# Multi-head projections between the first two latent groups, with the work of maxima, low parts and normalisation spread anew

## The chip, the core and the metric

The kernel runs on one core of one Trainium2 chip. Its time is the device time of one execution in microseconds (us), and the figure compared is the median of several runs. The profile is of one further execution.

## The reference

The input `x` has 8 batches of 256 rows of 256 features, in float32. It is normalised by row (a layernorm without weights) to `xn`, and two branches start from there:

- a latent attention with 16 heads, each with 16 content and 64 rotary features: `c_q = xn @ w_dq.T`, `c_kv = xn @ w_dkv.T`; queries and keys from these (rotary keys from `xn` directly), scores scaled by `1/sqrt(80)`, causal softmax, values, and the output weights: `s`;
- an ordinary attention with 16 heads of 16 features on `rmsnorm(xn)`, added to `xn` as a residual, and behind it a mixture of 8 experts of which each row takes two: `g = silu(...)`.

The result is `x + s * g`. Everything is float32; where the kernel splits a number into a high part that TensorE reads in one pass and a low remainder, the two add up to it.

## The kernel before

A program of one core, with an order written out by hand for each of the five engines; all waits are semaphores. First come the weights (they are multiplied out and split into high and low parts, to about 28 us), then the eight batches of both attentions and the routing (to about 600 us), then the experts. The change touches the first two parts.

A batch `b` passes three stages on TensorE. They overlap the engines' other work, and the stages of neighbouring batches are interleaved:

- **P1(b), the projections** (`stage_p1`, line 764, with `p1_with_m1`, line 957): thirteen units, in the order of `UNITS` (line 51): content queries and keys `nq`, `nk`, the rotary ones in four groups of four heads `q0` to `k3`, the multi-head ones `mq`, `mk`, and the latent values `v`. Each is twelve matmuls into one PSUM bank (`BANK`); a unit waits until its bank's last content was taken. After `nq` come the last values of the batch before and small transposes, after `k0` `to_tokens`, after `k1` `back`, after `k2` `project` (lines 714 to 741: the heads' way into tokens and through the output weights). After `k3` the first two heads of the maxima's scores.
- **T2(b-1), the multi-head attention** of the batch before (`stage_t2`, line 919, through `heads`, line 839), and in it the latent scores of batch `b` from which only row maxima are taken (`max1`, line 814): head `h + 2` behind the scores of head `h`. At its end the sixteen maxima are transposed (`max_t1`).
- **T1(b), the latent attention** (`stage_t1`, line 882), and in it in the same way the multi-head scores for their maxima (`max2`, line 830), in steps of heads, two of them ahead.

VectorE makes the rope products (`products`, line 1532: two instructions a unit, times cosine and times sine), POOL adds them (`rope_sums`, line 593), SyncE sends the sums into `qt` and `kt` by DMA (`place_rope`, line 440), and ScalarE rounds them there for the maxima's scores (`rounded`, line 1186). ScalarE also keeps `nq` and `nk`, takes all exponentials (`exps`, line 1251), and works strictly in the order of its program: P1's roundings stand ahead of T2's exponentials. For the multi-head queries and keys VectorE scales a unit (`mha_scale`, line 1545), ScalarE takes the high part (`mha_high`), VectorE the low part (`mha_low`, line 1554); SyncE stores the parts in HBM (`store_mha`, twelve DMAs: each high part goes to two places) and loads them back in the layout of the scores (`load_mha`, four DMAs for each half of the heads), once the scores of the batch before have let the half go.

All these pieces pass through one staging ring `stg` of five slots. `place` (line 98) gives each piece the next slot, in the order of `STAGED` (line 53), and the count at which its last user's DMAs have landed; who writes into a slot waits for that count.

The row of latent maxima goes from PSUM through `mt` (ScalarE, `max_t1`, line 1166) into the row `MROW` of `qt` by a DMA that SyncE issues (`row1`, line 410) between the two halves of `load_mha`. VectorE takes the maxima with two reducing instructions a head (`maxima`, line 1590). Between its products stand the normalisation of the heads behind the attention (`normalise` in `close_heads`) and routing steps (`position_steps`, `gate_steps`), put there by number: `after = {1: ..., 6: ...}` in `batch`, line 1601. The layernorm of `x` is applied for batch 0 ahead of its P1, and for the other seven behind the first seven product pairs of P1(0) (line 1761).

Of the kernel before, what the change touches and what calls it, by code (L numbers as in the profile page):

```python
# [23 lines left out]
F32 = mybir.dt.float32  # L24
# [19 lines left out]
G = 4  # L44
# [67 lines left out]
def build(nc, x, w_cols, w_dq, w_uqr, w_dkv, w_ukv, w_out, w_o, w_ln1, w_ln2, w_r, w_experts,  # L112
          cosines, sines, ident, mask, upper, route_c, slots, ones, out):
    ctx = ExitStack()
    with ctx:
# [276 lines left out]
        def _(sp):  # L392
# [17 lines left out]
            def row1(b):  # L410
                sp.wait_ge(mte1, b + 1)
                sp.dma_start(qt[MROW:MROW + 1, :, :], mt[:, :]).then_inc(md1, 16)

# [33 lines left out]
            def zero_rows():  # L447
                sp.wait_ge(clear, 2)
                for e in range(2):
                    sp.dma_start(mha_d[0, e, MROW2:ST, :, :], qt2[MROW2:ST, e, :, :].bitcast(F32)).then_inc(mzd, 16)  # L450

            def store_mha(b, a):
                for name, parts, ready in (((("mqh", (0, 1), hi2), ("mql", (2,), s2d)),
                                            (("mkh", (0, 2), hi2), ("mkl", (1,), s2d)))[a]):
                    s, _, _ = place(b, name)
                    sp.wait_ge(ready, 2 * b + a + 1)
                    for k in parts:
                        for e in range(2):
                            sp.dma_start(mha_d[a, e, D * k:D * (k + 1), :, :].rearrange("d (j t) s -> (d j) t s", t=2),  # L459
                                         stg[e * ST:(e + 1) * ST, s, :, :]).then_inc(sl[s], 16)  # L460

            def load_mha(b, t):
# [9 lines left out]
            def stage_p1(b, between):  # L472
# [11 lines left out]
                between()  # L484
                for t in range(2):
                    wait(sp, mrd[t], 64 * b)
                store_mha(b, 0)
                store_mha(b, 1)

            stage_p1(0, zero_rows)  # L490
# [3 lines left out]
            row1(0)  # L494
            for b in range(last):
# [4 lines left out]
                stage_p1(b + 1, lambda: store_s(b))  # L500
                load_mha(b + 1, 0)
                row1(b + 1)
# [64 lines left out]
        def _(pool):  # L567
# [116 lines left out]
        def _(pe):  # L684
# [79 lines left out]
            def stage_p1(b, after):  # L764

                free = dict(q0=(ex1, 16 * b), k0=(ex1, 16 * b), q1=(nkd, 2 * b + 1), k1=(nkd, 2 * b + 2),
                            q2=(roped, 8 * b + 1), k2=(roped, 8 * b + 2), q3=(roped, 8 * b + 3),
                            k3=(roped, 8 * b + 4), mq=(roped, 8 * b + 5), mk=(roped, 8 * b + 6), v=(roped, 8 * b + 7))
                for name in UNITS:
# [5 lines left out]
                    else:  # L775
                        wait(pe, *free[name])
                    if name == "mq" and b == 0:
                        pe.wait_ge(wdone, N_DIRECT)
# [25 lines left out]
            def max_t1(b):  # L804

                wait(pe, roped, 8 * b + 8)
# [1134 lines left out]
```

## Time and profile before

| what | us |
|---|---|
| median of 3 runs (lowest, highest) | 864.14 (859.2, 868.65) |
| profiled execution | 858.59 |
| its span, first to last instruction | 856.9 |
| busy in it: TensorE matmuls | 756.2 (88%) |
| TensorE weight loads (beside the matmuls) | 677.5 (79%) |
| VectorE | 556.7 (65%) |
| ScalarE | 437.9 (51%) |
| POOL | 378.7 (44%) |
| mean granted clock of TensorE, as a share of 2.4 GHz | 0.914 |

All engines run beside each other, so busy times do not add up to the span. Matmuls are pipelined and the ends that the profile gives them are modelled: a TensorE that is busy throughout need not be at its peak. The granted clock is either 1.00 or 0.50, and a value between is a mean over a stretch. Other names: PEld is the weight load, DVE VectorE, ACT ScalarE, SPq the instruction by which SyncE issues a DMA.

### The profile page before, as it was taken

The numbers are of one execution on the slowest core, as the hardware profiler recorded it, in microseconds if no ns is written. First come the engines' busy times: TensorE is split into PE (matmuls) and PEld (weight loads), VectorE is DVE, ScalarE is ACT, GpSimd is POOL, SyncE is SP. The second block draws the span as 40 slices with busy tenths as digits, with TensorE's granted clock in tenths as the row PEclk, the third lists the DMA queues.
The fourth block names the chain that finished last, engine by engine and source line by source line (L and its number), as shares of the span: only waits on it lengthen the run. The fifth ranks groups of instructions, "written<-read, shape, count | busy, mean of one in ns | idle before, by whom it ended". The sixth has DMA issues, their size and how long they took to land.

```text
span 856.9 us, 17025 instructions
## 1 busy us (share of the span) xinstructions
PE 756.2 (88%) x5968; PEld 677.5 (79%) x5968; DVE 556.7 (65%) x1933; ACT 437.9 (51%) x903; POOL 378.7 (44%) x473
## 2 busy tenths in 40 slices
PE   5856999999999999999999899888399999999980
PEld 3744897888888788888788789666299999999970
DVE  3785457657657657657657548633477888888854
ACT  2331337336436536436436435544167877778752
POOL 3440244234444444344344344424526566667640
PEclk9885599999999999999999999958599999999995
DMA  9346067347357347446447428724369999999836
GB/s 299 64 109 142 1 83 168 73 72 168 84 70 163 92 63 166 95 58 156 99 63 162 99 42 164 193 87 124 102 180 230 227 237 231 257 250 249 221 37 208
DMA packets 82952, 119.74 MB, mean 140 GB/s; under 512 B 16963, under 2 KB 57155, under 8 KB 82819
## 3 DMA queue, kind: packets, MB, share of 16 engines
q1 hardware_dynamic: 72148, 105.93, 51.4%
q0 software_dynamic: 9856, 12.13, 8.0%
q8 instruction: 47, 0.77, 0.4%
q10 hardware_dynamic: 864, 0.60, 0.3%
q14 instruction: 37, 0.30, 0.2%
HBM read 70.06 MB, written 27.66 MB: 114 GB/s over the span
## 4 chain that ended last, share of the span: by engine, by line
PE 67%; DVE 8%; DMA 7%; SPq 4%; issue 3%; ACT 2%; POOL 1%; DVEq 0%; POOLq 0%; ACTq 0%
PE ps L686 62%; DMA kt<-multi_heads 4%; SPq L459 3%; DVE ps L1596 1%; PE ps L1075 1%; SPq L469 1%; PE ps L722 1%; PE ps L731 1%; DVE ps L1593 1%; DMA multi_heads<-stg 1%; DVE ex L1543 1%; DMA qt<-mt 1%; DVE stg L1542 1%; DVE xr L1841 1%; DVE s_tok L1839 1%
## 5 line engine op out<-in xcount | busy, mean ns | idle before, releaser
L630 POOL TENSOR_SCALAR_AFFINE_SELECT ex<-ex 128x256 f32<-128x256 f32 x256 | 105.9, 417 | 228.4 <-ACT ex L1269 216.1
L1269 ACT ACTIVATE ex<-ps 128x384 f32<-128x384 f32 x240 | 115.7, 491 | 140.8 <-PE ps L686 138.6
L686 PE MATMUL ps<-qt,kt 81*128 81x128 f32 (+2 forms) x768 | 175.0, 343 | 9.6 <-ACT ex L1269 4.4
L1593 DVE CUSTOM_DVE_ANT_0 ps<-ps,mask 128x128 f32<-128x128 f32 x256 | 78.4, 306 | 108.9 <-PE ps L686 106.9
L686 PEld LDWEIGHTS ps<-qt,kt 81*128 81x128 f32 (+1 forms) x768 | 117.8, 207 | 21.4 <-issue 8.1
L599 POOL TENSOR_TENSOR stg<-stg,ex 128x512 f32<-128x512 f32 x64 | 83.5, 1305 | 95.7 <-DVE ex L1543 94.0
L1596 DVE CUSTOM_DVE_ANT_0 ps<-ps,mask 128x256 f32<-128x256 f32 x256 | 118.9, 464 | 0.0
L673 POOL DMA_INDIRECT expert_rows<-yo,slot_of x46 | 79.5, 1729 | 76.3 <-ACT yo L1393 47.8
L1430 DVE TENSOR_TENSOR wel<-raw,weh 128x768 fp32r<-128x768 f32 x92 | 87.7, 956 | 18.4 <-ACT weh L1128 18.4
L686 PE MATMUL ps<-xth,wh 128*128 128x256 f32 x384 | 82.4, 296 | 5.9 <-DVE ex L1543 3.0
L686 PE MATMUL ps<-kt,qt 128*128 128x128 f32 (+1 forms) x256 | 76.5, 389 | 11.3 <-DMA kt<-multi_heads 9.8
L686 PE MATMUL ps<-xeh,weh 128*128 128x256 f32 x368 | 78.3, 294 | 1.9 <-DVE xel L1820 1.9
L1542 DVE TENSOR_TENSOR stg<-ps,cos_t 128x512 f32<-128x512 f32 x64 | 43.9, 686 | 55.5 <-PE ps L686 53.9
L686 PE MATMUL ps<-xth,wl 128*128 128x256 f32 x384 | 77.5, 284 | 0.0
L686 PE MATMUL ps<-xtl,wh 128*128 128x256 f32 x384 | 77.4, 283 | 0.0
L1128 ACT ACTIVATE weh<-raw 128x768 fp32r<-128x768 f32 x92 | 77.0, 837 | 0.0
L686 PE MATMUL ps<-xel,weh 128*128 128x256 f32 x368 | 74.1, 283 | 0.0
L686 PE MATMUL ps<-xeh,wel 128*128 128x256 f32 x368 | 73.9, 282 | 0.0
L686 PEld LDWEIGHTS ps<-kt,qt 128*128 128x128 f32 x256 | 50.9, 210 | 22.3 <-DMA kt<-multi_heads 6.7
L686 PEld LDWEIGHTS ps<-xth,wh 128*128 128x128 f32 x384 | 60.6, 193 | 9.4 <-issue 5.3
L686 PE MATMUL ps<-kr,qr 80*128 80x128 f32 (+1 forms) x256 | 58.2, 322 | 7.8 <-DVE negm L1596 7.2
L662 POOL DMA_INDIRECT xg<-x_normalised,slot_of x46 | 55.2, 1201 | 18.6 <-issue 13.7
(157 smaller groups left out, 1679.5 us busy)
## 6 DMA issues: line engine op xcount, KB each, us to landing
raw<-in_w_experts SPq DMA_DIRECT2D x92, 384.0 KB, 4.5
multi_heads<-stg SPq DMA_DIRECT2D x96, 128.0 KB, 2.4
qt<-stg SPq DMA_DIRECT2D x64, 128.0 KB, 3.9
kt<-stg SPq DMA_DIRECT2D x64, 128.0 KB, 3.7
qt<-multi_heads SPq DMA_DIRECT2D x32, 256.0 KB, 4.9
kt<-multi_heads SPq DMA_DIRECT2D x32, 192.0 KB, 5.2
qt<-stg SPq DMA_DIRECT2D x8, 256.0 KB, 4.6
kt<-stg SPq DMA_DIRECT2D x8, 256.0 KB, 6.1
```

Of the source, the lines that this page charges most:

```text
L459: sp.dma_start(mha_d[a, e, D * k:D * (k + 1), :, :].rearrange("d (j t) s -> (d j) t s", t=2), stg[e * ST:(e + 1) * ST, s, :, :]).then_inc( ...
L599: nc.gpsimd.tensor_tensor(t, t, prb[:, n % 2, :, :], ALU.add).then_inc(tokd, 1)
L630: nc.gpsimd.affine_select(a, a, [[0, 2], [1, P]], ALU.is_ge, zero, 0, -1).then_inc(exm, 1)
L662: nc.gpsimd.indirect_dma_start(xg[:, blk % NXG, j, :], None, x2n[:, :], bass.IndirectOffsetOnAxis(mt_b[:, blk, j, 0:1], 0)).then_inc(xgd[b ...
L673: nc.gpsimd.indirect_dma_start(ys[:, :], bass.IndirectOffsetOnAxis(mt_b[:, blk, j, 1:2], 0), yo[:, blk % 2, j, :], None, compute_op=ALU.ad ...
L686: return nc.tensor.matmul(o, a, m, start=start, stop=stop, skip_group_check=True, **k)
L1128: return nc.scalar.activation(o, a, ACT.Copy)
L1269: nc.scalar.activation(ex[:, h % (2 * G), :], ps[4 + h % 2][:, P:4 * P], ACT.Exp, scale=scale).then_inc(ex_, 1)
L1430: return nc.vector.tensor_tensor(o, a, b.bitcast(F32), ALU.subtract)
L1542: nc.vector.tensor_tensor(stg[:, s, :, :], a, cos_t[:, :].unsqueeze(1).broadcast_to([P, 2, S]), ALU.mult)
L1593: nc.vector.tensor_tensor_reduce(out=o[:, 0:P], in0=o[:, 0:P], in1=mask2[:, 1, :], scale=-1.0, scalar=-2.0 * BIG, op0=ALU.add, op1=ALU.min ...
L1596: nc.vector.tensor_tensor_reduce(out=o[:, S:2 * S], in0=o[:, S:2 * S], in1=mask2[:, :, :].rearrange("p a k -> p (a k)"), scale=-1.0, scala ...
```

## The change

- `UNITS`, `BANK`, `STAGED`: `mq` and `mk` stand behind `k0` instead of behind `k3`, in the banks' order and in the staging ring.
- VectorE scales them there and goes on with q1; the products of q1 and k1 wait for the low parts, since the scaled values lie in their buffer.
- The low parts are taken by POOL, between the sums of k0 and q1, and not by VectorE.
- Each high part is stored once (eight DMAs for four pieces), and `load_mha` reads it into two places: eight DMAs for each half of the heads instead of four. The stores stand behind the first group's DMAs on SyncE's queue, ahead of the other three groups.
- Four heads of the latent maxima's scores, not two, stand in P1 (two after `k2`, one after `q3`, one after `k3`); in T2 the maxima run four, then three heads ahead, and are transposed one head earlier.
- `to_tokens` moves behind `mk`, `normalise` behind the products of q1, `project` from P1 into T2, behind the third head, and `kept` to the eighth head of T2's maxima.
- The row of latent maxima is sent by ScalarE, behind its own copy.
- The rounding of the last group of queries goes from ScalarE to VectorE.
- `x` is normalised two tiles at a time, in T1 behind the fourth head of the batch before, instead of all in P1(0).
- At the start TensorE no longer waits for the masks and for two of the low weights before `nq`; `rms_rows(0)` stands behind `nk`, and the multi-head values of batch 0 behind its transposed maxima.

```diff
-UNITS = ("nq", "nk", "q0", "k0", "q1", "k1", "q2", "k2", "q3", "k3", "mq", "mk", "v")
-BANK = dict(nq=0, nk=1, q0=4, k0=5, q1=0, k1=1, q2=4, k2=5, q3=0, k3=1, mq=4, mk=5, v=0)
-STAGED = dict(nq=1, nk=1, q0=2, k0=2, q1=2, k1=2, q2=2, k2=2, q3=2, k3=2, mqh=4, mql=2, mkh=4, mkl=2)
+UNITS = ("nq", "nk", "q0", "k0", "mq", "mk", "q1", "k1", "q2", "k2", "q3", "k3", "v")
+BANK = dict(nq=0, nk=1, q0=4, k0=5, mq=0, mk=1, q1=4, k1=5, q2=0, k2=1, q3=4, k3=5, v=0)
+STAGED = dict(nq=1, nk=1, q0=2, k0=2, mqh=2, mkh=2, mql=2, mkl=2, q1=2, k1=2, q2=2, k2=2, q3=2, k3=2)
+EARLY = 4
...
             def load_mha(b, t):
...
                 for e in range(2):
-                    for a, o, n in ((0, qt2[:, e, :, :], ST), (1, kt2, MROW2)):
-                        sp.dma_start(o[ST * e:ST * e + n, 4 * t:4 * (t + 1), :].bitcast(F32),
-                                     mha_d[a, e, 0:n, 4 * t:4 * (t + 1), :]).then_inc(mrd[t], 16)
+                    for a, o, parts in ((0, qt2[:, e, :, :], ((0, D, 0), (D, ST, 0))),
+                                        (1, kt2, ((0, 2 * D, 0), (2 * D, MROW2, 0)))):
+                        for r0, r1, d0 in parts:
+                            sp.dma_start(o[ST * e + r0:ST * e + r1, 4 * t:4 * (t + 1), :].bitcast(F32),
+                                         mha_d[a, e, d0:d0 + r1 - r0, 4 * t:4 * (t + 1), :]).then_inc(mrd[t], 16)
...
                 place_content(b, 0)
                 place_content(b, 1)
-                for g in range(NG):
+                place_rope(b, 0, 0)
+                place_rope(b, 0, 1)
+                if b == 0:
+                    zero_rows()
+                for t in range(2):
+                    wait(sp, mrd[t], 128 * b)
+                store_mha(b, 0)
+                store_mha(b, 1)
+                for g in range(1, NG):
                     place_rope(b, g, 0)
                     place_rope(b, g, 1)
...
                 for n in range(2 * NG):
+                    if n == 2:
+                        mha_low(b, 0)
+                        mha_low(b, 1)
                     wait(pool, roped, 8 * b + n + 1)
...
+            def mha_low(b, a):
+
+                s, free, _ = place(b, ("mql", "mkl")[a])
+                wait(pool, sl[s], free)
+                pool.wait_ge(hi2, 2 * b + a + 1)
+                sh, _, _ = place(b, ("mqh", "mkh")[a])
+                nc.gpsimd.tensor_tensor(stg[:, s, :, :].bitcast(F32R), prb[:, a, :, :], stg[:, sh, :, :],
+                                        ALU.subtract).then_inc(s2d, 1)
...
-                wait(pe, xnd, 2 if b == 0 else TT)
+                wait(pe, xnd, 2 * b + 2)
...
-                    if h + 2 < H:
-                        max_head(h + 2)
-                    if h == H - 1:
+                    if h in ahead:
+                        max_head(ahead[h])
+                    if h == H - 2:
                         tail()
...
-                stage_p1(b, after | {"k3": first_heads})
+                stage_p1(b, after | {"k2": lambda: (head(0), head(1)), "q3": lambda: head(2), "k3": lambda: head(3)})
...
-                    p1_with_m1(b + 1, {"nq": after_first, "k0": between, "k1": back, "k2": project})
-                    stage_t2(b, max1(b + 1), {5: lambda: project_v2(b + 1)})
+                    p1_with_m1(b + 1, {"nq": after_first, "mk": between, "k1": back})
+                    stage_t2(b, max1(b + 1), {2: project, 5: lambda: project_v2(b + 1)})
...
-            p1_with_m1(0, {"q1": lambda: rms_rows(0)})
-            project_v2(0)
-            for h in range(2, H):
+            p1_with_m1(0, {"nk": lambda: rms_rows(0)})
+            for h in range(EARLY, H):
                 max1(0)(h)
             max_t1(0)
+            project_v2(0)
...
                 copy(mt[:, :], ps[1][0:H, 0:S]).then_inc(mte1, 1)
+                wait(act, mte1, b + 1)
+                act.dma_start(qt[MROW:MROW + 1, :, :], mt[:, :]).then_inc(md1, 16)
...
                 if b > 0:
+                    mha_high(b, 0)
+                    mha_high(b, 1)
                     keep_back(b - 1, fb1, of1, o1)
                 else:
                     rms_rows(b)
-                for g in range(RING):
-                    rounded(b, g, 0)
-                    rounded(b, g, 1)
-                mha_high(b, 0)
-                mha_high(b, 1)
+                    mha_high(b, 0)
+                    mha_high(b, 1)
+                rounded_q(b, 0)
+                rounded_k(b, 0)
+                for g in range(1, RING):
+                    rounded_q(b, g)
+                    rounded_k(b, g)
...
                 wait(dve, sl[s], free)
                 if n == 0:
                     wait(dve, pv1, NG * b)
-                wait(dve, tokd, 8 * b + n - 1)
+                if n in (2, 3):
+                    dve.wait_ge(s2d, 2 * b + n - 1)
+                else:
+                    wait(dve, tokd, 8 * b + n - 1)
...
             def stage_p1(b, after):
-                for n in range(2 * NG):
+                products(b, 0)
+                products(b, 1)
+                mha_scale(b, 0)
+                mha_scale(b, 1)
+                for n in range(2, 6):
                     products(b, n)
                     after.get(n, lambda: None)()
-                first_m1(b)
-                mha_scale(b, 0)
-                mha_scale(b, 1)
-                mha_low(b, 0)
-                mha_low(b, 1)
+                wait(dve, mtr1, b)
+                max1(b, 0)
+                max1(b, 1)
+                products(b, 6)
+                max1(b, 2)
+                products(b, 7)
+                max1(b, 3)

             def stage_m1(b, after):
-                wait(dve, mtr1, b)
-                for h in range(2, H):
-                    maxima(b, h, h, negm1, m1d, mx1)
+                for h in range(EARLY, H):
+                    if h == 12:
+                        rounded_q(b, 3)
+                    max1(b, h)
                     after.get(h, lambda: None)()
...
-                    after = {1: normalise, 6: kept, 13: lambda: x_low(b + 1)}
+                    after = {1: normalise, 3: lambda: normalised_two(b + 1), 6: kept, 13: lambda: x_low(b + 1)}
...
-                    after = {1: normalise, 6: kept}
+                    after = {2: normalise}
                     if not first:
...
-                        after = {1: lambda: (normalise(), in_expert()), 2: chosen, 3: lambda: (summed(), plus_one()),
-                                 4: lambda: (marked(), stepped()), 5: inverse, 6: lambda: (both(), kept())}
+                        after = {2: lambda: (normalise(), in_expert(), chosen()), 3: lambda: (summed(), plus_one()),
+                                 4: lambda: (marked(), stepped()), 5: lambda: (inverse(), both())}
                     stage_p1(b + 1, after)
-                    stage_m1(b + 1, {})
+                    stage_m1(b + 1, {7: kept})
...
-            stage_p1(0, {n: lambda n=n: normalised_two(n + 1) for n in range(7)})
-            dve.wait_ge(xnd, TT)
+            stage_p1(0, {})
             stage_m1(0, {})
```

## Rows read from the trace of the kernel before

**Rows 1.** Windows: us, busy (x count) PE, PEld, DVE, ACT, POOL; granted clock; DMA.

```profile
57.90:81.96 24.06, 13.82 (x47) 10.53 (x47) 13.24 (x70) 4.15 (x7) 2.26 (x1) 0.50 0.78 165
...
370.75:394.23 23.48, 23.48 (x209) 22.72 (x206) 16.11 (x44) 9.64 (x15) 10.62 (x9) 1.00 0.60 102
394.23:412.68 18.45, 15.88 (x141) 12.60 (x139) 10.75 (x58) 12.04 (x27) 6.79 (x16) 0.91 0.73 168
...
412.68:436.05 23.37, 22.33 (x180) 19.20 (x180) 16.23 (x88) 10.50 (x23) 10.78 (x21) 1.00 0.25 61
```

**Rows 2.** Chain of waits in one P1: start, us, what.

```profile
373.79 4.21 PE ps L686 x36
...
381.89 0.44 PE ps L731 x4
```

**Rows 3.** Timeline of VectorE in P1: start, us, line, operation, idle before and releaser.

```profile
182.34 0.69 DVE L1542 TENSOR_TENSOR stg<-ps,cos_t 128x512 f32<-128x512 f32 x1 [6.00 <-PE ps L686]
...
376.74 0.69 DVE L1542 TENSOR_TENSOR stg<-ps,cos_t 128x512 f32<-128x512 f32 x1 [5.99 <-PE ps L686]
...
378.14 0.69 DVE L1542 TENSOR_TENSOR stg<-ps,cos_t 128x512 f32<-128x512 f32 x1
...
379.35 0.36 DVE L1502 RECIPROCAL rec<-ps 128x16 f32<-128x16 f32 x2
...
380.62 0.69 DVE L1542 TENSOR_TENSOR stg<-ps,cos_t 128x512 f32<-128x512 f32 x1
...
385.42 1.12 DVE L1712 TENSOR_SCALAR rc<-rc 128x8 f32<-128x8 f32 x1
```

**Rows 4.** Timeline of TensorE: `project` in P1, third head of T2, next batch's first scores.

```profile
384.98 1.89 PE L686 MATMUL ps<-wo,otf 128*128 128x256 f32 x8
...
395.62 0.50 PE L686 MATMUL ps<-qt,kt 128*128 128x256 f32 x2 [0.26 <-ACT ex L1269]
396.87 0.47 PE L686 MATMUL ps<-kr,qr 80*128 80x128 f32 x2 [0.74 <-DVE negm L1596]
...
412.68 0.73 PE L686 MATMUL ps<-kt,qt 128*128 128x128 f32 x4 [1.25 <-DMA kt<-multi_heads]
```

**Rows 5.** Timeline of VectorE in P1(0): two tiles of x normalised.

```profile
36.41 1.71 DVE L370 TENSOR_SCALAR xn<-xn,mv,rstd 128x256 f32<-128x256 f32 x2
```

**Rows 6.** Timeline of SyncE's queue: the two DMAs of k0 issued.

```profile
380.82 1.19 SPq L445 DMA_DIRECT2D kt<-stg  x2
```

**Rows 7.** DMAs issued near 407.3, 391.7, 41.4: KB, us from issue to landing.

```profile
kt<-multi_heads SPq DMA_DIRECT2D x1, 192.0 KB, 5.3
...
qt<-stg SPq DMA_DIRECT2D x1, 128.0 KB, 3.2
...
kt<-stg SPq DMA_DIRECT2D x1, 128.0 KB, 3.3
```

**Rows 8.** Timeline of ScalarE: k0 rounded in two batches, k2, both high parts.

```profile
191.60 1.07 ACT L1128 ACTIVATE kr<-kt 80x1024 fp32r<-80x1024 f32 x1 [0.59 <-DMA kt<-stg]
...
387.47 1.07 ACT L1128 ACTIVATE kr<-kt 80x1024 fp32r<-80x1024 f32 x1 [2.02 <-DMA kt<-stg]
...
393.09 1.06 ACT L1128 ACTIVATE kr<-kt 80x1024 fp32r<-80x1024 f32 x1
394.06 1.14 ACT L1128 ACTIVATE stg<-ex 128x512 fp32r<-128x512 f32 x2
```

**Rows 9.** Timeline of POOL: power for `rms_rows(0)`, two sums of P1.

```profile
32.13 1.40 POOL L602 TENSOR_TENSOR rms<-msq,mhalf 128x2 f32<-128x2 f32 x1 [0.70 <-DVE msq L1751]
...
378.11 2.69 POOL L599 TENSOR_TENSOR stg<-stg,ex 128x512 f32<-128x512 f32 x2 [7.08 <-DVE ex L1543]
```

**Rows 10.** Chain of waits ahead of the first T1: maxima heads, row of maxima.

```profile
64.38 0.78 PE ps L686 x2
...
72.60 0.81 PE ps L686 x2
75.97 5.95 DMA qt<-mt
```

More of the change, by code:

```diff
@@ L449, in zero_rows, with store_mha @@
                 for e in range(2):
[L450 to L460, printed above, removed]
+                    sp.dma_start(mha_d[0, e, 2 * D:3 * D, :, :], qt2[MROW2:ST, e, :, :].bitcast(F32)).then_inc(mzd, 16)
+            def store_mha(b, k):
+                for a in range(2):
+                    s, _, _ = place(b, ("mqh", "mkh", "mql", "mkl")[2 * k + a])
+                    sp.wait_ge((hi2, s2d)[k], 2 * b + a + 1)
+                    for e in range(2):
+                        sp.dma_start(mha_d[a, e, D * k:D * (k + 1), :, :].rearrange("d (j t) s -> (d j) t s", t=2),
+                                     stg[e * ST:(e + 1) * ST, s, :, :]).then_inc(sl[s], 16)
             def load_mha(b, t):
@@ L480, in stage_p1 @@
                 place_content(b, 1)
-                for g in range(NG):
+                place_rope(b, 0, 0)
[7 more added lines that the diff above has]
+                for g in range(1, NG):
                     place_rope(b, g, 0)
                     place_rope(b, g, 1)
[L484 to L490, printed above, removed]
+            stage_p1(0)
             sp.wait_ge(mzd, 32)
@@ L776, in stage_p1 @@
                         wait(pe, *free[name])
+                    if name == "k0" and b == 0:
+                        pe.wait_ge(wdone, 1)
+                        pe.wait_ge(wdonep, 1)
                     if name == "mq" and b == 0:
@@ L804, in max_t1 @@
             def max_t1(b):
-                wait(pe, roped, 8 * b + 8)
+                wait(pe, roped, 8 * b + 6)
                 max_t(b, ps[1], negm1, mx1, mtr1)
@@ L832, in head @@
                     if h % 8 == 0:
-                        wait(pe, mrd[h // 8], 64 * (b + 1))
+                        wait(pe, mrd[h // 8], 128 * (b + 1))
                     if h >= 2:
@@ L837, in max2, with heads @@
                 return head
-            def heads(b, scores_t, st, ex_, exm, pv, ov_, v, before_h0, before_pv0, max_head, tail, after):
+            def heads(b, scores_t, st, ex_, exm, pv, ov_, v, before_h0, before_pv0, max_head, ahead, tail, after):
                 before_h0()
@@ L887, in before_h0 @@
                     wait(pe, v1d, b + 1)
-                return heads(b, scores1, st1, ex1, exm1, pv1, ov1, v1, before_h0, lambda: wait(pe, x2d, b), max2(b), lambda: None, after)
+                return heads(b, scores1, st1, ex1, exm1, pv1, ov1, v1, before_h0, lambda: wait(pe, x2d, b), max2(b),
+                             {h: h + 2 for h in range(H - 2)}, lambda: None, after)
             def last_t2(after):
@@ L895, in last_t2 @@
                 heads(last, scores2, st2, ex2, exm2, pv2, ov2, v2, before_h0, lambda: pe.wait_ge(ov1, NG * last + 2),
-                      lambda h: None, lambda: None, after)()
+                      lambda h: None, {}, lambda: None, after)()
             def latent_head(h):
@@ L923, in before_h0 @@
                     wait(pe, v2d, b + 1)
-                    wait(pe, m2p, 2 * (b + 1) + 2)
-                heads(b, scores2, st2, ex2, exm2, pv2, ov2, v2, before_h0, lambda: wait(pe, sd, b + 1), max_head,
+                    wait(pe, roped, 8 * (b + 1) + 8)
+                ahead = {h: h + EARLY for h in range(8)} | {h: h + 3 for h in range(9, 13)}
+                heads(b, scores2, st2, ex2, exm2, pv2, ov2, v2, before_h0, lambda: wait(pe, sd, b + 1), max_head, ahead,
                       lambda: max_t1(b + 1), after)()
@@ L1184, in landed, with rounded_q, rounded_k @@
                 act.wait_ge(sl[s], done)
-            def rounded(b, g, a):
-                landed(b, ("nq", "nk")[a])
-                landed(b, "qk"[a] + str(g))
+            def rounded_q(b, g):
+                landed(b, "nq")
+                landed(b, "q" + str(g))
                 wait(act, m1d, G * (NG * b + g - RING + 1))
-                o, t, done = ((qr, qt, rrd), (kr, kt, rkd))[a]
-                copy(o[0:HW, (NG * b + g) % RING, :, :], t[0:HW, G * g:G * (g + 1), :]).then_inc(done, 1)
+                copy(qr[0:HW, (NG * b + g) % RING, :, :], qt[0:HW, G * g:G * (g + 1), :]).then_inc(rrd, 1)
+            def rounded_k(b, g):
+                landed(b, "nk")
+                landed(b, "k" + str(g))
+                wait(act, m1d, G * (NG * b + g - RING + 1))
+                copy(kr[0:HW, (NG * b + g) % RING, :, :], kt[0:HW, G * g:G * (g + 1), :]).then_inc(rkd, 1)
             def keep_content(b, a):
@@ L1267, in exps @@
                     if h == 5:
-                        wait(act, s2d, sums)
+                        wait(act, tokd, sums)
                     nc.scalar.activation(ex[:, h % (2 * G), :], ps[4 + h % 2][:, P:4 * P], ACT.Exp,
```

55 lines of the change are left out of this document (22 added, 33 removed).

## The prediction

> **What bounds the kernel now.** Windows by stage come first. In one of the seven like batches TensorE is busy through the whole of its projections (P1, from 370.75), for 15.9 of 18.5 us in the multi-head scores behind them (T2, from 394.23), and for 22.3 of 23.4 in the next batch's latent scores (T1); no other engine comes near that [rows 1]. So time is won or lost where TensorE waits or its clock falls. The chain of waits and the engines' timelines show where. Three units of P1 take 4.21 us, 1.40 each, and the transposes `back` follow at 381.89 without a pause [rows 2]. VectorE keeps pace: q0's products start at 376.74, k0's at 378.14, a pair of them lasts 1.21, q1's start at 380.62 [rows 3]. The pauses lie at the borders: T2 halts at its third head, 0.26 and 0.74, and the next batch opens with 1.25 for the multi-head load [rows 4]; T2's mean granted clock of 0.91 [rows 1] stands for 3.3 us at 1.2 GHz instead of 2.4. Ahead of the first batch there is another kind of time: 81.9 us until the first latent scores, with TensorE idle for 10 of the last 24 and at a granted clock of 0.50 [rows 1], and VectorE normalising two tiles of x (1.71) after each of seven product pairs [rows 5].
>
> **The load at a batch's start.** Storing mq and mk early ends the 1.25 us, unless the load, now eight issues instead of four, comes late: at 0.6 an issue [rows 6] the last starts 4.2 us in and lands 5.3 later [rows 7], 9.5 in all, against the half of T2 (some 8.5 us by the sum below) that follows its release. I take the 1.25 as gained; 1.0 of it may return.
>
> **The staging ring, the largest term.** Five slots serve in the order of `STAGED`, so each tile waits until the one five places ahead has landed. In the new order q1 stands five behind k0 of its own batch; before, five ahead of it was a tile of the batch before. Everything up to k0 is unchanged on all queues, so the trace shows when k0 lands: its two DMAs are issued from 380.82 [rows 6], and ScalarE's copy of k0, released by them, starts at 387.47, that is 10.7 us after q0's products; in another batch it is 9.3 [rows 3, 8]. These are the longest and the shortest of the seven. Their mean is 9.9. VectorE needs the slot before q1's products: 376.74 + 9.9 = 386.6 instead of 380.62. The two scalings of mq and mk, and k0's successors on other queues, fit into that gap at no cost; the low parts, 1.35 each on POOL if they go like its sums [rows 9], end before it.
>
> **What queues behind.** `normalise` is now put behind q1's products: 386.6 + 1.21 + 1.27 (with the next small step [rows 3]) = 389.1. TensorE reaches `back` two units later than before, at 381.89 + 2.8 = 384.7, and idles there for about 4.3. Then `back` 0.44 and q2 1.40 [rows 2]: q2's products run from 390.8 to 392.0. `stepped` follows with 1.12 [rows 3]; k2's products end at 394.3.
>
> The Trainium skill, SBUF — State Buffer, section "Who interferes with whom", says that VectorE's tensor_scalar (in a two-port mode) and a GpSimd instruction hold one port pair exclusively and the loser blocks for the whole instruction. That speaks against giving POOL more to do in P1. By it `stepped`, a tensor_scalar behind a pair's products, waits out the whole of a POOL sum, 1.35 instead of 1.12, and the sum below would be 0.2 per batch longer; its 1.12 for eight columns agrees so far.
>
> From k2's products: sum 1.35, second issue 0.6 after the first, 3.2 to landing [rows 6, 7, 9]: 394.3 + 1.35 + 0.6 + 3.2 = 399.5. Here ScalarE rounds k2; before it did so at 393.09 [rows 8]. In its queue all of T2's exponentials stand behind this copy. Two copies of high parts, 1.14, have left the place between [rows 8], so T2's third head comes 6.4 - 1.1 = 5.3 later: 400.9 instead of 395.62.
>
> **The rest of T2.** From the third head to the next batch were 17.06 us. Off go the load's 1.25 and, with four maxima ahead, the pause of 0.74; `project` comes in from P1 with 1.89 [rows 4]. I give no credit for the two maxima that left T2. 16.96 remain, the next batch starts at 417.9 instead of 412.68: **5.2 us lost** per batch. I leave T2's drop of the clock in. Bounds: without the drop 1.6 less (half of 3.3). TensorE's idle prologue ran at 0.50 [rows 1]; if the idle 4.3 at `back` costs as much clock as T2 loses now, 1.6 more. If k0 lands 3.3 after its second issue, as in the prologue [rows 7], 1.9 less. So 1.7 to 7.8, with 1.0 for the load on top. Seven batches, of which the first has no routing steps (1.1 less): 7 x 5.2 - 1.1 = 35.3, bounds 11 to 61.
>
> **x by batch.** In the loop a pair costs VectorE at most the 1.71 of [rows 5], in T1, where it waits for TensorE anyway (16.2 of 23.4 us busy [rows 1]); if that cover is gone, 1.7 per batch. I cost it at nothing.
>
> **The prologue.** Seven pairs of 1.71 go, 12.0. Against it: `rms_rows` behind nk waits for POOL until 32.13 + 1.40 = 33.5 [rows 9], so at half clock (2.8 a unit) q0 is ready at 36.3 and k0 at 39.1. k0's products end at 40.3, its sum at 41.7, it lands at 42.3 + 3.3 = 45.6 [rows 7]; from there the ring lets q1, k1, q2, k2 through one store apart (1.4), k2's products ending at about 51.0. Four maxima at 0.82 (ten heads in 8.22 us [rows 10]) and the pairs of q3 and k3 bring it to 56.7, twelve more heads to 66.5, q3's rounding on VectorE (1.07 on ScalarE [rows 8]) to 67.6. The multi-head values at half clock, 2.8, follow: 70.4, then two heads of scores: 71. The row of maxima is the other condition.
>
> On it the Trainium skill, DMA: Bandwidth & Descriptors, section "Issuing engines are not separate DMA queues", speaks against the change: whichever engine issues, the transfers share the same 16 engines, and only issue time is saved. By it the row would take the 5.95 it took before.
>
> The trace has that row behind the eight loads [rows 10]; if it stays behind them, 67.6 + about 1 for its copy and issue + 5.95 = 74.5 opens T1. So T1 starts at 71 to 74.5 instead of 81.9; I take 9.5 gained, bounds 7.5 to 11. In the steady batches the pause is the load's, so I count nothing there for sending the row by ScalarE.
>
> **Sum.** 35.3 - 9.5 = 25.8 on the profiled 858.59 (span 856.9): 884.4. The three runs have their median 5.5 above the profiled one; I put the forecast between, at **886**. Its own range is 866 to 904: the bounds all at one end would give 11 - 11 = 0 and 61 - 7.5 = 53, 859 to 912, less likely together than singly.
>
> **Rivals.** (1) *q1's slot is no wait*: k0 lands before q1 is projected (383.2). That is 1.8 us from its second issue; the quickest landings here are 3.2 and 3.3 [rows 7]. Then everything behind comes 3.4 earlier, 1.8 lost per batch, 7 x 1.8 - 1.1 - 9.5 = 2: **861 to 866**, no change. Chance 0.16, with the cases where the bounds at the low end come together.
> (2) *Faster: T2 runs at TensorE's own pace.* Place: from the third head on. With four maxima ahead neither maxima nor exponentials hold it up. T2's weight loads are busy for 12.6 us now [rows 1], 11 at full clock, and `project` makes that about 12 of the 16.96. Price: 5 us per batch, 35 in all, so 35.3 - 35 - 9.5 = -9: **850**, less if k0 also lands early. It decides once T2 takes under 12 us from its third head. For it: T2's pauses [rows 4] and slow clock. Against it: ScalarE begins its sixteen exponentials behind the late rounding and is then the one that is followed. Chance 0.16.
> (3) *The stall costs more*: the clock falls at `back` and in T2, or the load is late again: 7.7 per batch, **905**. Chance 0.18, on top of 0.50 for the forecast.
>
> **Chances.** A difference of 1% (8.6 us) is about what a measurement of this kernel can tell from none. Slower by over 1%: the forecast and (3), 0.68. Within 1%: (1) and a part of (2), 0.18. Faster: the rest of (2), 0.14. The range of 8 in 10 runs from 851, where (2) begins, to 908.
>
> **What would show it.** In the changed profile: VectorE's first instruction for q1 idle before it, released by the DMA of k0 into `kt`, about 9.9 after q0's; `back` waiting for `otk` by 4 us; T2's third head released by ScalarE some 30 us after P1's start instead of 25; no wait for the multi-head load; T1 of the first batch at 71 to 74. The forecast is wrong if q1's products start at once, or if T2 is shorter than 13 us from its third head.

## The result and the profile after

The change makes the kernel slower: 896.95 us (median; 892.16 to 902.89) against 861.67 for the kernel before, run beside it; ratio 1.040, 95% interval 1.031 to 1.050. The profiled execution took 895.67 with a span of 893.9, 37.0 more than before's.

The stages, taken from the timelines by TensorE's first matmul of each, divide the 37.0. The second P1 begins at 97.99 instead of 110.32: 12.3 gained. From P1 to the next T1 the seven batches take 343.0 instead of 293.3: 49.7 lost, 7.1 per batch. From T1 to P1 six of them take 1.2 more; behind the last T1 1.6 is gained. The windows of one batch (columns as in [rows 1]; last 24 us ahead of the first latent scores, P1, T2, T1):

```profile
49.55:73.61 24.06, 16.64 (x71) 14.16 (x71) 16.93 (x79) 6.20 (x8) 8.87 (x6) 0.61 0.82 155
387.35:421.08 33.73, 26.52 (x205) 25.57 (x202) 18.07 (x50) 10.56 (x16) 11.87 (x10) 0.87 0.48 98
421.08:437.87 16.79, 15.42 (x144) 11.92 (x143) 9.57 (x52) 9.88 (x23) 7.39 (x17) 1.00 0.48 116
437.87:461.75 23.88, 22.90 (x184) 19.31 (x180) 16.73 (x90) 10.86 (x24) 11.15 (x21) 0.98 0.22 48
```

P1 was TensorE's throughout [rows 1]; now it is 10.3 us longer and 7.2 of them idle, at a granted clock of 0.87. T2 is 1.7 shorter. The waits (engine, line, what it waited for: us in total, times, longest) name two idle times of TensorE and one of VectorE:

```profile
PE ps L742 <- DVE otk L1529: 35.0, 13, 5.6
DVE stg L1567 <- DMA kt<-stg: 33.9, 8, 5.0
...
PE ps L697 <- DVE negm L1629: 22.7, 13, 4.1
```

VectorE's timeline in that P1 (start, us, line, operation, idle before and releaser), to be held against [rows 3]:

```profile
394.16 0.69 DVE L1567 TENSOR_TENSOR stg<-ps,cos_t 128x512 f32<-128x512 f32 x1 [7.49 <-PE ps L697]
...
404.08 0.69 DVE L1567 TENSOR_TENSOR stg<-ps,cos_t 128x512 f32<-128x512 f32 x1 [5.04 <-DMA kt<-stg]
...
405.68 0.75 DVE L1529 TENSOR_TENSOR otk<-ps,rec 128x256 f32<-128x256 f32 x2
...
410.15 0.69 DVE L1567 TENSOR_TENSOR stg<-ps,cos_t 128x512 f32<-128x512 f32 x1 [1.90 <-PE ps L697]
...
411.70 1.14 DVE L1745 TENSOR_SCALAR rc<-rc 128x8 f32<-128x8 f32 x1
412.75 0.68 DVE L1567 TENSOR_TENSOR stg<-ps,cos_t 128x512 f32<-128x512 f32 x1
...
414.13 1.26 DVE L1448 COPY meta<-gsum 128x2 f32<-128x2 f32 x1
...
415.38 0.28 DVE L1626 CUSTOM_DVE_ANT_0 ps<-ps,mask 128x128 f32<-128x128 f32 x1
```

TensorE's, for [rows 2, 4]:

```profile
406.49 1.12 PE L742 MATMUL ps<-idf,otk 128*128 128x128 f32 x4 [4.39 <-DVE otk L1529]
407.26 0.78 PE L697 MATMUL ps<-xth,wh 128*128 128x256 f32 x2
...
411.29 0.63 PE L697 MATMUL ps<-kr,qr 80*128 80x128 f32 x4
...
416.16 0.51 PE L697 MATMUL ps<-kr,qr 80*128 80x128 f32 x2 [2.82 <-DVE negm L1629]
...
422.12 0.50 PE L697 MATMUL ps<-qt,kt 128*128 128x256 f32 x2
...
437.08 0.86 PE L697 MATMUL ps<-ex,v 128*32 128x256 f32 x16 [1.00 <-POOL ex L641]
```

ScalarE, where k2 is rounded and T2's exponentials begin, for [rows 8]:

```profile
419.03 1.06 ACT L1139 ACTIVATE kr<-kt 80x1024 fp32r<-80x1024 f32 x1 [1.33 <-DMA kt<-stg]
...
421.58 0.49 ACT L1292 ACTIVATE ex<-ps 128x384 f32<-128x384 f32 x1 [1.49 <-PE ps L697]
```

Read in order: q1's products (404.08) wait 5.04 for k0's landing; `normalise` stands behind them, so TensorE waits 4.39 at `back`; `back` and most of q2 then run at half clock (its four transposes take 1.12; 0.60 in the timeline before, 0.44 in the chain of [rows 2]). VectorE goes through q2, a small step (`stepped`, 411.70), k2, and another small step (414.13) to the first head's maxima (415.38). TensorE's scores for the third head's maxima ("the third pair" below) have waited 2.82 for their result. So TensorE comes late to T2, and its third head there (422.12) waits for nobody.

POOL in the same stretch (its two low parts, two sums):

```profile
400.03 1.30 POOL L609 TENSOR_TENSOR stg<-ex,stg 128x512 fp32r<-128x512 f32 x1 [1.80 <-DMA kt<-stg]
401.83 1.26 POOL L609 TENSOR_TENSOR stg<-ex,stg 128x512 fp32r<-128x512 f32 x1 [0.51 <-DMA qt<-stg]
...
411.52 1.29 POOL L601 TENSOR_TENSOR stg<-stg,ex 128x512 f32<-128x512 f32 x1 [2.08 <-DVE ex L1568]
...
414.11 1.26 POOL L601 TENSOR_TENSOR stg<-stg,ex 128x512 f32<-128x512 f32 x1 [1.30 <-DVE ex L1568]
```

VectorE's copy of 128x2, the second small step, lasts from 414.13 to 415.39, POOL's last sum here from 414.11 to 415.37. More of that at the end.

### The profile page after: what moved, and what is told of

Its sections match the earlier page's. It is cut to its first block, busy times and chain, and to the rows that moved or that the text cites. A ratio compares the mean times of both kernels' runs of the same rounds, so it can differ in the third digit from the quotient of the medians.

```text
span 893.9 us, 17047 instructions
## 1 busy us (share of the span) xinstructions
PE 766.2 (86%) x5968; PEld 683.5 (76%) x5968; DVE 551.4 (62%) x1925; ACT 430.3 (48%) x895; POOL 389.5 (44%) x489
## 4 chain that ended last, share of the span: by engine, by line
PE 65%; DVE 13%; DMA 8%; issue 5%; ACT 4%; POOL 4%; SPq 1%; ACTq 0%; DVEq 0%; POOLq 0%
PE ps L697 61%; DMA kt<-stg 4%; DVE ex L1568 2%; ACT ex L1292 2%; DVE stg L1567 2%; DVE ps L1629 2%; POOL stg L601 2%; DVE ps L1626 1%; DMA expert_rows<-yo,slot_of 1%; PE ps L1086 1%; PE ps L742 1%; DVE otk L1529 1%; DMA w_ukv_raw<-in_w_ukv 1%; SPq L442 1%; DVE xr L1873 1%
## 5 line engine op out<-in xcount | busy, mean ns | idle before, releaser
L641 POOL TENSOR_SCALAR_AFFINE_SELECT ex<-ex 128x256 f32<-128x256 f32 x256 | 103.4, 407 | 192.9 <-ACT ex L1292 181.1
L697 PE MATMUL ps<-qt,kt 81*128 81x128 f32 (+2 forms) x768 | 169.7, 336 | 5.2 <-issue 2.2
L697 PEld LDWEIGHTS ps<-qt,kt 81*128 81x128 f32 (+1 forms) x768 | 112.8, 199 | 17.6 <-issue 8.7
L684 POOL DMA_INDIRECT expert_rows<-yo,slot_of x46 | 76.0, 1652 | 82.1 <-ACT yo L1415 49.2
L1567 DVE TENSOR_TENSOR stg<-ps,cos_t 128x512 f32<-128x512 f32 x64 | 44.0, 687 | 105.6 <-PE ps L697 67.4
L697 PE MATMUL ps<-xth,wh 128*128 128x256 f32 x384 | 87.7, 313 | 1.5 <-issue 1.5
L697 PE MATMUL ps<-xth,wl 128*128 128x256 f32 x384 | 84.4, 305 | 0.0
L697 PE MATMUL ps<-xtl,wh 128*128 128x256 f32 x384 | 83.9, 303 | 0.0
L697 PE MATMUL ps<-xel,weh 128*128 128x256 f32 x368 | 74.5, 284 | 0.0
L697 PEld LDWEIGHTS ps<-xth,wh 128*128 128x128 f32 x384 | 67.0, 215 | 4.5 <-issue 4.4
L697 PEld LDWEIGHTS ps<-xtl,wh 128*128 128x128 f32 x384 | 67.1, 214 | 0.0
L697 PEld LDWEIGHTS ps<-xth,wl 128*128 128x128 f32 x384 | 67.0, 214 | 0.0
```

What stands on the lines that cost most here:

```text
L641: nc.gpsimd.affine_select(a, a, [[0, 2], [1, P]], ALU.is_ge, zero, 0, -1).then_inc(exm, 1)
L684: nc.gpsimd.indirect_dma_start(ys[:, :], bass.IndirectOffsetOnAxis(mt_b[:, blk, j, 1:2], 0), yo[:, blk % 2, j, :], None, compute_op=ALU.ad ...
L697: return nc.tensor.matmul(o, a, m, start=start, stop=stop, skip_group_check=True, **k)
L1567: nc.vector.tensor_tensor(stg[:, s, :, :], a, cos_t[:, :].unsqueeze(1).broadcast_to([P, 2, S]), ALU.mult)
```

## The experiments

"P1 to T1" is the sum over the seven batches, measured as above, in the profiled execution: 293.3 before, 343.0 after. Each ratio is to the kernel before, run beside the experiment.

**1. Multi-head tiles out of the ring.** The four tiles go into the part of `ex` (the exponentials' buffer) that is free in P1, and the first exponential of a stage waits until they are stored; the ring keeps five slots for the other ten tiles.

```diff
-STAGED = dict(..., k0=2, mqh=2, mkh=2, mql=2, mkl=2, q1=2, ...)
+STAGED = dict(..., k0=2, q1=2, ...)
+mh_t = ex[:, :, :].rearrange("p h c -> p (h c)")[:, 0:8 * S].rearrange("p (n a s) -> p n a s", n=4, a=2)
```

> The changed kernel, with the four multi-head tiles taken out of the ring into memory that the exponentials leave free in P1; q1 then stands five behind the v... the last tile of the batch before, and no longer behind k0. Ring theory: q1's products start when POOL's first low part is done, about 13.0 us after P1's start instead of 15.1 to 16.7; normalise comes 3.5 earlier, TensorE's wait at the transposes `back` falls from 4.4 to about 0.9, the clock holds there, and all seven batches lose some 5 us less: 35 less, about 862. Rival A (the wait moves on to the low parts on POOL, whose products hold q1's buffer): q1's products no earlier than 15, 890 or more. Rival B (TensorE's stall at the third pair of maxima is what the batch pays): wait at `back` gone, but the stall grows by as much, 885 to 897.

874.98, ratio 1.015 (1.006 to 1.025); P1 to T1 318.5. q1's products start 12.5 to 12.7 after P1's start in five batches, and 14.2 in the two where q0's come at 7.5 instead of 6.0. TensorE, batch at 237.5:

```profile
252.62 0.66 PE L738 MATMUL ps<-idf,otk 128*128 128x128 f32 x4 [1.14 <-DVE otk L1525]
...
260.83 0.49 PE L693 MATMUL ps<-kr,qr 80*128 80x128 f32 x2 [2.77 <-DVE negm L1625]
```

The ring's wait and most of the one at `back` are gone, and 24.5 of the 49.7 with them, not 35: the stall at the third pair stays as it was. The theory was right in kind and too large in size.

**2. `normalise` ahead of q1's products.**

```diff
                 mha_scale(b, 1)
+                after.get(1, lambda: None)()
                 for n in range(2, 6):
...
-after = {2: lambda: (normalise(), in_expert(), chosen()), ...
+after = {1: normalise, 2: lambda: (in_expert(), chosen()), ...
```

> The changed kernel, with VectorE's normalise put ahead of q1's products; the ring is as it was, so q1's products still wait for k0's landing. Theory: normalise is what TensorE idles for; its wait at `back` goes to zero, the clock does not fall there, q2 and k2 are projected while VectorE waits, and q2's products come 3.6 us earlier; 7 x 3.6 = 25 less, about 872. Rival (the ring wait itself, not what stands behind it, sets the batch, since the rounding of k2 follows q1's products): under 1.5 less per batch, 887 or more.

889.2, ratio 1.030 (1.021 to 1.039); P1 to T1 335.0, 1.1 per batch less. Waits of TensorE:

```profile
PE ps L697 <- DVE negm L1630: 41.1, 12, 5.3
...
PE ps L742 <- DVE otk L1529: 8.8, 7, 5.6
```

The wait at `back` lost 26.2, and the one at the third pair took up the larger part (18.4). The rival held: VectorE begins q1 no earlier, and TensorE waits for it one place further on.

**3. TensorE kept busy ahead of `back`** with three useless projections of q2.

```diff
+                    def filled_back():
+                        wait(pe, m2p, 2 * (b + 1) + 1)
+                        for _ in range(3):
+                            features(ps[0][:, 0:S], COLS["q2"])
+                            features(ps[0][:, S:2 * S], COLS["q2"] + P)
+                        back()
```

> The changed kernel, with q2's projection done three times over, uselessly, just ahead of `back`, so that TensorE is busy for 4.2 us where it idled for 4.4; nothing else waits less. Clock theory: the granted clock holds through `back`, q2, k2 and the first heads, q2 and k2 last 1.4 each instead of 2.6 and 1.45, and a batch is 1.2 to 2.0 shorter: 8 to 14 less, 883 to 889. Rival (the idle time costs itself alone): within 3 us of 897, or some us more where the filling overruns the wait.

893.56, ratio 1.037 (1.031 to 1.044); by the times alone this is the same as the changed kernel. In the traces P1 to T1 is 334.0, 9.0 less, or 1.3 per batch: the clock's part as expected. The second P1 begins at 102.0 here and at 98.0 in the changed kernel's profile, which takes 4.0 of it back.

**4. The kernel before with x by batch alone** (the three places of the diff that concern `xnd` and `normalised_two`).

```diff
-wait(pe, xnd, 2 if b == 0 else TT)
+wait(pe, xnd, 2 * b + 2)
...
-stage_p1(0, {n: lambda n=n: normalised_two(n + 1) for n in range(7)})
+stage_p1(0, {})
```

> The kernel before, with one part of the change alone: x is normalised two tiles at a time inside the batches instead of all of it between the first batch's products. Theory: most of the prologue's gain is this; T1 of the first batch opens about 9 us earlier, batches from then on are as before: 850 to 854. Rival A (the gain needs the earlier rows of mean squares and the earlier sent row of maxima too): 3 us at most, 859. Rival B (in the loop the pair of 1.71 is no longer covered): 7 x 1.7 given back, 862 to 866.

858.69, ratio 0.999 (0.994 to 1.005). The first latent scores come at 75.73 instead of 81.96, the second P1 at 108.25 instead of 110.32. TensorE there, and windows of this kernel and then of the kernel before and the changed one (last columns: granted clock, DMA share, GB/s):

```profile
75.73 1.65 PE L686 MATMUL ps<-qt,kt 81*128 81x128 f32 x4 [4.49 <-DMA qt<-mt]
```

```profile
100.00:105.00 5.00, 5.00 (x28) 4.17 (x21) 1.87 (x9) 1.25 (x3) 0.81 (x2) 0.50 0.00 0
105.00:110.00 5.00, 5.00 (x33) 3.42 (x32) 0.10 (x2) 1.37 (x3) 0.81 (x2) 0.58 0.00 2
```

```profile
100.00:105.00 5.00, 5.00 (x20) 4.48 (x18) 1.69 (x10) 1.25 (x3) 0.82 (x3) 0.50 0.01 3
105.00:110.00 5.00, 5.00 (x49) 3.60 (x51) 2.76 (x13) 3.09 (x7) 1.63 (x4) 0.93 0.00 0
```

```profile
85.00:90.00 5.00, 5.00 (x33) 3.67 (x32) 1.48 (x8) 1.08 (x3) 0.81 (x2) 0.62 0.00 0
90.00:95.00 5.00, 5.00 (x46) 4.30 (x46) 3.65 (x17) 2.75 (x7) 1.62 (x4) 1.00 0.01 3
```

The theory's 850 to 854 was missed. The opening is 6.2 earlier, but all of T1(0) runs at 1.2 GHz and the clock rises only at about 109, although TensorE does not pause from 75.73 on; before, it rose at about 105.6, in the changed kernel at about 89. So in this profile little is left of the opening. Experiment 10 has the same edit: there the clock rose at about 98, and the second P1 begins at 102.56, 7.8 earlier than before. What the opening is worth hangs on when the clock rises, and that differs from profile to profile. In the loop T1 lasts 23.4 to 23.5, no longer than before: rival B fell. The row of maxima, sent by SyncE behind the loads, is what the opening waits for, as rival A had it in kind.

**5. Experiments 1 and 2 together.**

> The kernel of the first experiment (the multi-head tiles out of the ring), and normalise ahead of q1's products as in the second. Theory (TensorE's idle time at `back` is paid in full): the 1.1 us that are left of that wait go, a batch is 1.1 to 1.5 shorter, about 865 to 867. Rival (the stall at the third pair of maxima, set by VectorE's queue, takes what is gained ahead of it): that stall grows from 2.8 to about 4, the batch stays at 45.0, 873 to 877.

876.02, ratio 1.016 (1.003 to 1.029); P1 to T1 313.5, or 44.8 per batch. The rival held: the stall at the third pair grew.

```profile
331.29 0.49 PE L693 MATMUL ps<-kr,qr 80*128 80x128 f32 x2 [3.56 <-DVE negm L1626]
```

**6. Experiment 1 with two heads in P1** (`EARLY = 2`, the third and fourth head back in T2, two ahead).

> The kernel of the first experiment, with two heads of maxima in the projections instead of four: the third and fourth go back into T2, with VectorE's and TensorE's parts of them. Theory: what is left of the loss, 3.2 us per batch, is TensorE's 2.8 at the third pair of maxima, which in P1 stands in front of k3 and v; without it a batch is 2 to 3 shorter, 43 or less from P1 to T1, about 856 to 860. Rival (the wait only moves to T2's third head, as in the kernel before): batches of 44.5 to 45, 871 or more.

891.56, ratio 1.036 (1.026 to 1.045); P1 to T1 323.4, or 46.2 per batch: slower than experiment 1 by 17. The theory fell. The rival's time (871 or more) holds, but not its place and not its 44.5 to 45 per batch. The stall of P1 turns up at T2's start, where TensorE now waits for k3's products, and there is a second wait, which experiment 1 does not have. VectorE rounds the last group of queries ahead of the thirteenth head's maxima; TensorE, only two heads ahead now, waits for that in each of the seven batches:

```profile
410.46 0.47 PE L693 MATMUL ps<-qt,kt 128*128 128x256 f32 x2 [3.03 <-DVE ex L1564]
...
424.08 0.49 PE L693 MATMUL ps<-kr,qr 80*128 80x128 f32 x2 [1.16 <-DVE qr L1444]
```

T2's granted clock is 0.85 to 0.91 here, 1.00 in experiment 1. Only 4.9 of the 17 lie between P1 and T1; T1 to P1 takes 6.0 more, and 5.9 lie behind the last T1; why stays open. So taking the two heads back in this form is slower. That the four early maxima cost nothing is not shown by it, since the edit brings a wait of its own.

**7. Experiment 1 with the small routing steps at T2's end.**

```diff
-3: lambda: (summed(), plus_one()), 4: lambda: (marked(), stepped()), 5: lambda: (inverse(), both())}
+3: lambda: (summed(), plus_one()), 4: marked}
...
+late_steps |= {14: stepped, 15: lambda: (inverse(), both())}
```

> The kernel of the first experiment, with four maxima in P1 as in the change, but the small routing steps of VectorE (stepped 1.15; inverse and both 1.43) moved from P1 to the end of T2. Theory: they stand ahead of the first two maxima in VectorE's queue, and the third head of TensorE waits for these; 2.58 less in front of them shortens the stall from 2.8 to about 0.3, 6 of 7 batches are 2.3 shorter, 859 to 862. Rival (VectorE's products for k2, themselves late, set the stall): the stall stays above 1.5, 867 or more.

871.25, ratio 1.014 (1.008 to 1.020); P1 to T1 320.1 (in an execution of 878.01, the longest of the five). The stall at the third pair went as expected; the time hardly fell. TensorE and ScalarE, batch at 381.6:

```profile
402.28 0.49 PE L693 MATMUL ps<-kr,qr 80*128 80x128 f32 x2 [0.15 <-DVE negm L1625]
...
410.60 0.80 PE L693 MATMUL ps<-qt,kt 128*128 128x256 f32 x2 [2.90 <-ACT ex L1288]
...
411.62 3.61 PE L693 MATMUL ps<-wo,otf 128*128 128x256 f32 x8
```

```profile
409.12 1.06 ACT L1135 ACTIVATE kr<-kt 80x1024 fp32r<-80x1024 f32 x1 [0.70 <-DMA kt<-stg]
410.08 0.47 ACT L1288 ACTIVATE ex<-ps 128x384 f32<-128x384 f32 x1
```

T2's third head now waits 2.90 for an exponential, which stands behind the rounding of k2, 27.5 after P1's start where it was 22.3 before [rows 8]; `project` behind it takes 3.61 instead of 1.89, at half clock. This is the wait that the prediction named. The stall ahead of it had hidden it.

**8. Experiments 1, 2 and 7 together.**

> The seventh's edit and normalise ahead of q1's products, on the kernel of the first: ring, `back` and routing steps all mended, four maxima kept. Theory: no wait of TensorE over 1 us is left in P1; P1 to T1 takes 41 to 42 as before or less, the prologue's gain stays, 845 to 855. Rival (T2 then is held by the late rounding of k2 or by the low clock): 43 or more from P1 to T1, 858 to 865.

875.07, ratio 1.016 (1.008 to 1.024); P1 to T1 322.3 (in an execution of 882.5). The rival's range lies lower, but its mechanism is the one seen: TensorE waits 21.5 in all for exponentials, 20.6 of it at T2's third head.

**9. Experiment 8 with the roundings of q2 and k2 behind T2's second and third exponential.**

```diff
-{0: lambda: keep_v1(b + 1), 7: lambda: rounded_k(b + 1, 3),
+{0: lambda: keep_v1(b + 1), 1: lambda: rounded_q(b + 1, 2), 2: lambda: rounded_k(b + 1, 2), 7: lambda: rounded_k(b + 1, 3),
```

> The eighth kernel, with ScalarE's roundings of q2 and k2 moved from in front of T2's exponentials to behind the second and third of them (TensorE needs them from T2's fifth head on). Theory: in the eighth, T2's third head waits 2.9 for an exponential that stands behind the rounding of k2, which lands 3 us later than before because mq and mk are projected ahead of q1, k1, q2 and k2; TensorE's clock falls behind that wait. Without it the clock holds, P1 to T1 takes 41 to 42.5 instead of 45 to 47, 850 to 856. Rival (the landing of k2 still holds T2, now at its fifth head): 44 or more, 868 or more.

839.91, ratio 0.972 (0.958 to 0.985); P1 to T1 288.4. **Faster than both kernels**, and better than expected. The profiled execution took 844.54; its span is 14.1 shorter than before's. Of that 8.8 lie ahead of the second P1, 4.9 between P1 and T1. T2's granted clock is 1.00 in all seven batches; before it was 0.90 or 0.91 in six of them. From the batch at 360.9, up to T2's last values, two short waits are left:

```profile
382.22 0.50 PE L693 MATMUL ps<-kr,qr 80*128 80x128 f32 x2 [0.84 <-DVE negm L1627]
...
387.25 0.47 PE L693 MATMUL ps<-kr,qr 80*128 80x128 f32 x2 [0.91 <-issue]
```

**10. The kernel before with x by batch and the same later roundings.**

> The kernel before, with x by batch (the fourth experiment) and the same move of ScalarE's roundings of q2 and k2 into T2; the order of the units is that of before. Theory: the third head's pause and the fall of the clock behind it (1.0 and 1.6 in a batch of before) go, P1 to T1 takes 39 to 40 instead of 41.8, about 840 to 846. Rival (the load of the multi-heads or the fourth group's landing holds T2's end): 41 or more, 855 or more.

852.42, ratio 0.992 (0.986 to 0.998); P1 to T1 293.0, as before. The theory fell. The third head no longer waits in six of the seven batches, but TensorE waits at the maxima behind it, 0.56 to 1.53 in all seven, once for the rounding of q2 that had been moved:

```profile
260.13 0.47 PE L686 MATMUL ps<-kr,qr 80*128 80x128 f32 x2 [1.41 <-ACT qr L1128]
```

T2's granted clock is again 0.90 or 0.91 in five of the seven. Of the rival, the 41 or more per batch holds; its 855 lies 3 too high, and the load of the multi-heads holds T2's end no longer than before (9.0 in all against 9.8). What the execution gains over before's lies in the opening: the second P1 begins at 102.56. So in the order of before the later roundings gain nothing in the loop, where experiment 9 gains 4.9. Which part of the change that is owed to, the early `mq` and `mk` or another, is not shown.

**11. Experiment 9 with the tiles back in the ring.**

> The ninth kernel with the multi-head tiles back in the ring of five, so that q1's products wait for k0's landing again; normalise first, gates late and the later roundings stay. Theory: the ring's wait is paid by all that follows q1's products: they start at 15.2 instead of 12.7 after P1's start, k2's at 20.6 instead of 18.1, and a batch is 2.5 longer than in the ninth: 840 + 7 x 2.5 = 857. Rival A (with nothing of TensorE's queued behind it the wait is hidden): 840 to 846. Rival B (the ring alone makes the 5 us per batch of the forecast): 872 or more.

866.5, ratio 1.0005 (0.997 to 1.004); P1 to T1 306.3, which is 17.9 more than in 9, or 2.6 per batch (2.5 expected). The two profiled executions are 22.7 apart, so 4.8 lie in other stages; the medians are 27 apart. The third pair waits again:

```profile
PE ps L697 <- DVE negm L1631: 25.7, 13, 4.1
DVE stg L1568 <- DMA kt<-stg: 25.3, 8, 3.8
```

**12. The changed kernel with the low parts on VectorE**, behind the two scalings.

> The changed kernel with the low parts of mq and mk computed on VectorE again, behind the two scalings, where VectorE waits 5 us for q1's slot; POOL does the sums alone. Theory: k0's landing sets q1's products either way, so the place of the low parts costs and gives nothing: within 6 us of the changed kernel's 897. Rival (POOL's low parts, 1.3 each, hold the sums and through them the batch): 1 to 2 less per batch, 883 to 890.

901.25, ratio 1.042 (1.033 to 1.050); P1 to T1 341.5 against 343.0. The place of the low parts costs and gives nothing; the rival fell.

## Why the prediction was right, and where its sizes were not

**Load wait**: right. No wait for the multi-head load is left; T2 ends in a wait of 1.00 for POOL.

**Ring**: right. q1's products come 9.92 after q0's in this batch, where 9.9 was predicted as a mean; that it fits to the tenth here is luck, the mean of the seven is 9.3 (9.1 to 9.9). Taken away, the ring's wait gives 3.5 per batch (experiment 1), or 2.6 where all else is mended (11 against 9). Rival 1 fell.

**`normalise` behind it**: right; the wait at `back` is 4.39 (4.3 predicted), 3.6 to 4.4 in the seven.

**"Then `back` 0.44 and q2 1.40"**: the first term that was too small. Behind the idle time `back` and most of q2 ran at half clock, and q2's products came 6.1 after q1's instead of 4.2. The prediction had this as a bound (1.6) and in rival 3; experiment 3 measured 1.3 per batch.

**"T2's third head comes 5.3 later"**: the second. From P1's start to that head it is 31.0 to 34.8, 33.0 in the mean, where 30 was predicted (0.5 of the difference lies ahead of q0's products). In the first batch, which has no routing steps, ScalarE still sets it, as predicted; in the other six the third pair of maxima in P1 does. The sum credited the four maxima with T2's pause of 0.74 and charged nothing for them in P1: the third pair waits for the first head's maxima on VectorE, which stand behind k2's products and two small routing steps, of which only the first was counted. The chain through k2's rounding was real, and comes next: with the stall gone it took its place at nearly the same price (experiment 7), and only with both gone the time fell, by 35 (9 against 8).

**Rest of T2**: 16.0 in the mean from the third head on (16.96 predicted). T2's fall of the clock, which the sum left in, is gone in six of the seven batches (granted clock 1.00). Rival 2 fell.

**x by batch**: right, nothing in the loop (experiment 4).

**Prologue**: the first latent scores at 73.61, inside 71 to 74.5, so 8.35 gained (9.5 predicted). The other 4 of the 12.3 came from the clock, which rose earlier in T1(0), and that was luck: in ten of the twelve experiments, with the same prologue, the second P1 begins at 101.5 to 105.2, so 5 to 9 is what to expect of it.

**Low parts on POOL**: right, they end at 403.1, ahead of k0's landing; nothing hangs on them (experiment 12).

**Bounds**: one sum is wrong. The 61 counts the load's 1.0 twice: 7 x 7.8 - 1.1 is 53.5. The 49.7 measured from P1 to T1 lie inside either.

So the forecast stood 10.95 below the measured 896.95, which lies between it and rival 3; that rival's fall of the clock at `back` occurred, its late load did not. The loop lost 14.4 more than its 35.3, and the opening gained 2.8 more than its 9.5.

**The Trainium skill's two rules.** SBUF — State Buffer, "Who interferes with whom": by it a copy, too, can block for the whole of a GpSimd instruction. The trace agrees, and it weighed more than the prediction gave it (0.2 per batch): the copy took 1.26 instead of 0.16; see below. DMA: Bandwidth & Descriptors, "Issuing engines are not separate DMA queues": by it the row of maxima would have taken 5.95 again. Here it was issued at 70.72 by ScalarE, 1.3 after the last load, and its reader started at 73.61, under 2.9 us later. With ScalarE it took 4.84 in experiment 1 and 3.9 to 4.8 in the nine others with this opening, with SyncE 5.95 in experiment 4 and 7.2 in experiment 10. So the row came sooner each time that ScalarE issued it, which goes against the Trainium skill's rule. That the queue alone does it is not shown: the loads ahead differ as well.

## What to carry to other kernels

A unit moved forward shifts every tile behind it in a ring: count which tile now stands a ring's length ahead, and when that one lands. Behind the first wait list the next ones in order, each with its engine's queue: here mending one of four waits uncovered the next, three mended gave no more than one, and all four gave 57 us. Compare the result with the kernel before by stages, too: the best version's gain over it lies more in the opening (8.8) than in the loop (4.9). A work item that is placed early for one engine is paid for where another engine's queue makes it wait.

## What the runs showed of the hardware

**A copy of two columns can take 1.26 us.** In the kernel before it ran in a pause of POOL (last sum up to 389.11, next from 389.79) and took 0.16:

```profile
389.62 0.16 DVE L1426 COPY meta<-gsum 128x2 f32<-128x2 f32 x1
```

After the change it begins inside a POOL sum and ends 0.02 after it, and lasts 1.26 in all six P1s that have routing steps; `stepped` likewise (1.14 here). In experiment 7, moved to where POOL does no sums, `stepped` took 0.17 in all six batches, and the copy 0.17 in three, this one among them, and 0.42 in three, where it ended 0.02 after a short POOL instruction:

```profile
425.42 0.17 DVE L1444 COPY meta<-gsum 128x2 f32<-128x2 f32 x1
```

VectorE's products, tensor_tensor of 512 columns with one input in PSUM, took 0.68 beside the same sums.

**The clock can stay low while TensorE does not pause.** Around T1(0) TensorE ran without a pause at a granted clock of 0.50 for some 33 us in experiment 4, some 24 before, and 19 in the changed kernel (counted from its last pause, at 69.7). In twelve of the fourteen profiles the rise came within or at the edge of a run of sixteen matmuls of the values (`ps<-ex,v`): the first such run in the changed kernel, the second in the eleven others. In experiments 4 and 8 it came about 1 us behind the third, when P1's products had begun. What sets the moment stays open.
